# A latent-attention, delta-rule and expert layer on one core: gate factors made ahead of the applications, centred key weights

## The chip, the cores and the metric

One core of a Trainium2 chip runs the whole program in one launch. The metric is the device time of an execution in microseconds, as the median of several runs of the same kernel. All tensors are fp32. A product that needs more than one pass of TensorE is split: an operand becomes a high half (a ScalarE copy to `fp32r`) and a low half (VectorE or GpSimd subtracts), and three matmuls per product are made (lines 103 to 105).

## The reference

512 latent rows (8 batches of 64) attend to 8 x 1601 context rows; a gated delta rule follows, then a layer of 8 experts with 2 chosen per row. What the change touches:

```
# cross attention: keys of the context, 8 groups of 128, layer norm per group
k = LN(ctx @ Wk.T) * kxln_w + kxln_b          # mean and variance over the 128 of a group
scores = q @ k.T / sqrt(128); p = softmax(scores); o = p @ v

# delta rule, chunk of 64 = all rows of one batch; 32 value heads, 16 key heads, d = 128
q = l2norm(q) * 128**-0.5; k = l2norm(k); g = cumsum(gate)         # g: one value per row and head
decay = where(lower, exp(g[:,None] - g[None,:]), 0)
A     = where(strict, -(beta*k) @ k.T * decay, 0)
v_c   = solve(I - A) @ (beta*v)                                     # state is zero: one chunk
o     = where(lower, q @ k.T * decay, 0) @ v_c
out   = (rmsnorm(o) * norm_w * silu(z)) @ w_out
```

## The kernel before

The stages follow one another on each of the five queues: stage 1 (projections of the latents, 0 to 157 us of the profile), 1b (self attention and the loads for stage 3, to 201), 3 (cross attention, to about 1800), 4 (its projection), 5 (delta rule, 1850 to 2364), 7 (gate and output projection, to 2472), 8 (experts).

**Stage 1b** works in 8 lots. Per lot TensorE turns the probabilities (`self_turn_pe`), makes the scores of the lot three ahead and the values; VectorE (`s1b_dv`) takes sums and scaling of lot k+1, maxima and subtraction of lot k+3, and in lots 1 to 4 the low half of one quarter of the key weights `wkr`; ScalarE (`s1b_ac`) evicts probabilities and outputs, and in lots 0 to 3 writes the high half `wkh`. The first matmul of stage 3 waits for all of `wkl` and for lot 7.

**Stage 3** runs over 8 batches. In each, 13 tiles of up to 128 context rows are projected to 8 x 128 keys (24 matmuls of 128x512). `kx_stats_dv` (VectorE) takes `bn_stats` and `bn_aggr` per group and adds the epsilon; GpSimd raises to -0.5; `kx_norm_ac` normalises groups 0 to 3 on ScalarE (with `nmr` = -mean/std from `kx_nmr_dv`), `kx_norm_dv` groups 4 to 7 on VectorE, one instruction per group. Then TensorE turns the tile. Behind the 13 tiles stand 8 score blocks with softmax and values; the first tile of the next batch is laid between the last tiles and score block 0, and the values of block 0 wait for that tile's norm (`kn_ac`, `kn_dv`).

**Stage 5** is one written-out order of steps, `stage_order`, which all queues walk; each queue acts on the steps that are its own, in that order.

- 96 positions `mm`, each a chunk of 128 output columns: 64 convolution chunks and 32 gate chunks. ScalarE makes the high half, GpSimd (`qkv_split_po`, convolution chunks) or VectorE (`gz_split_dv`, gate chunks) the low half, two positions ahead. VectorE convolves with three instructions from PSUM.
- 32 `build`s of four heads. TensorE makes k.k and q.k, ScalarE scales them into `kqs`, GpSimd adds the mask `negm` and -g of the column's row to the row of gates in `gb`, ScalarE's `decay` takes exp, GpSimd multiplies the factor `b` (beta and norm) with k.k; VectorE's `second` writes q.k x decay into `aq` and b x decay into `at_of(n)`, which SP stores to `at_d` (`coupling_store`). `gb` is loaded by `gate_load`, a broadcast over 64 partitions of `gb_d`, in pairs of builds; `gb_d` holds g and b with 64 rows per run. Builds 0 to 15 come in four bursts at positions 42 to 76, builds 16 to 31 in the applications.
- Four solves, one per 64 systems, numbered 0 to 3: `system` loads the 32x32 diagonal blocks from `at_d`, VectorE makes 31 pairs of `tensor_tensor` (lines 2169, 2172), `solved` stores the inverses to `z_d`. Solve 0 and 1 run beside the positions, 2 and 3 in the applications.
- The applications: 32 groups of four heads in rounds t = 0 to 35. A group passes p0 (inverse blocks `xt`, fetched from `z_d`), p1 (coupling `mt`, fetched from `at_d`; VectorE adds), p2 (inverse again), p3 (`aq`), each 8 matmuls; group n makes p0 in round n, p1 in n+1, and so on. Between them lie the builds, solve steps (`some`, with a budget), `square` (sums of squares for the norm, ScalarE, four instructions with accumulator per group) and `rms`. p3 is scaled by `rq` and evicted by ScalarE for groups 0 to 19, by VectorE from 20 on.

The solve steps are paced so:

```
def some(steps, n):
    while n > 0 and (step := next(steps, None)) is not None:
        yield step
        n -= 180 + step[2] * (32 - step[2])
```

## Time and profile before

| | |
|---|---|
| runs | 2776.19, 2776.43, 2780.57 us (median 2776.43) |
| profiled execution | 2779.4 us; its span 2777.6 us, granted TensorE clock 0.982 |
| busy | PE 2646.0 us (95%), DVE 1861.7 (67%), ACT 1574.0 (57%), POOL 504.8 (18%) |
| DMA | 317.91 MB, 116 GB/s of HBM traffic over the span; 128712 of 255061 packets under 512 B |
| chain that ended last | PE 79%, DVE 10%, ACT 4%, the rest issue, DMA and queues |

PE is TensorE's matmuls, PEld its weight loads, DVE VectorE, ACT ScalarE, POOL GpSimd, SP the queue that issues nearly all transfers. A row's line (L2169) is that of the kernel; `cv<-at_d` at L1815 is the load of the systems (they lie in a part of `cv`), `lnw` at L2169 is the solve's scratch. Busy time says little by itself; the question at each place is which wait ends last.

### The profile page before, as it was taken

How to read it: one execution, taken by the hardware profiler on the slowest of the kernel's cores; microseconds unless marked ns; L12 is line 12 of the kernel's file. 1: busy time of each engine (PE TensorE's matmuls, PEld its weight loads, DVE VectorE, ACT ScalarE, POOL GpSimd, SP SyncE). 2: the span in 40 equal slices, each digit the busy share in tenths (PEclk: the TensorE clock that was granted, in tenths of full speed). 3: DMA queues.
4: the chain of work that ended last, by engine and by line, in shares of the span. 5: the costliest groups of instructions: out<-in, count | busy, mean ns of one | idle time of the engine just before them, and what ended most of it. 6: DMA issues, size and time to landing. Idle time of an engine off the chain costs nothing.

```text
span 2777.6 us, 39649 instructions
## 1 busy us (share of the span) xinstructions
PE 2646.0 (95%) x13810; PEld 2194.4 (79%) x13810; DVE 1861.7 (67%) x4737; ACT 1574.0 (57%) x2992; POOL 504.8 (18%) x428
## 2 busy tenths in 40 slices
PE   6889999999999999999999999999999879999999
PEld 5778788887887887887887887878877768777887
DVE  7747648548547557457466476668669866668997
ACT  7945436436436445445345355437676567857776
POOL 4402002002002012011011020005353332022111
PEclk9989999999999999999999999999999999989999
DMA  3433013022022031031030121445676642549996
GB/s 125 137 123 86 10 55 93 15 67 75 17 79 61 20 88 46 24 94 30 24 99 20 40 84 50 132 140 156 177 211 168 158 94 66 187 184 368 376 371 228
DMA packets 255061, 317.91 MB, mean 114 GB/s; under 512 B 128712, under 2 KB 166216, under 8 KB 241808
## 3 DMA queue, kind: packets, MB, share of 16 engines
q1 hardware_dynamic: 251392, 310.03, 36.0%
q0 software_dynamic: 3040, 5.08, 0.7%
q8 instruction: 112, 1.84, 0.3%
q14 instruction: 85, 0.70, 0.1%
q10 hardware_dynamic: 432, 0.27, 0.0%
HBM read 274.22 MB, written 46.98 MB: 116 GB/s over the span
## 4 chain that ended last, share of the span: by engine, by line
PE 79%; DVE 10%; ACT 4%; issue 2%; DMA 2%; POOL 1%; SPq 1%; POOLq 0%; DVEq 0%; ACTq 0%
PE ps L103 20%; PE ps L105 20%; PE ps L104 20%; PE ps L874 3%; PE ps L830 3%; PE ps L902 2%; DVE lnw L2169 2%; DVE zz L2172 2%; PE ps L855 1%; DVE cv L2136 1%; PE ps L895 1%; PE ps L1344 1%; PE ps L1343 1%; PE ps L2010 1%; PE ps L579 1%
## 5 line engine op out<-in xcount | busy, mean ns | idle before, releaser
L1244 POOL TENSOR_TENSOR lnw<-lnw,half 128x8 f32<-128x8 f32 x88 | 144.4, 1641 | 1217.6 <-DVE lnw L964 1217.6
L103 PE MATMUL ps<-whf,cth 128*128 128x512 f32 (+1 forms) x832 | 336.1, 404 | 1.8 <-ACT kn L1117 1.8
L103 PE MATMUL ps<-cnh,pth 128*128 128x512 f32 (+1 forms) x832 | 329.9, 397 | 6.4 <-issue 6.4
L105 PE MATMUL ps<-whf,ctl 128*128 128x512 f32 (+1 forms) x832 | 325.9, 392 | 0.0
L104 PE MATMUL ps<-cnl,pth 128*128 128x512 f32 (+1 forms) x832 | 324.9, 390 | 0.0
L104 PE MATMUL ps<-wlf,cth 128*128 128x512 f32 (+1 forms) x832 | 324.9, 390 | 0.0
L105 PE MATMUL ps<-cnh,ptl 128*128 128x512 f32 (+1 forms) x832 | 324.6, 390 | 0.0
L2662 DVE TENSOR_TENSOR ml<-mr,mh 128x2048 fp32r<-128x2048 f32 x90 | 203.3, 2286 | 26.5 <-ACT mh L2604 26.5
L1155 ACT ACTIVATE pr<-ps,sm 128x1601 f32<-128x1601 f32 x56 | 89.6, 1600 | 205.7 <-DVE sm L1017 205.7
L1180 ACT ACTIVATE xo<-ps 128x128 f32<-128x128 f32 x64 | 17.7, 277 | 312.9 <-PE ps L902 312.9
L1036 DVE TENSOR_TENSOR ptl<-ps,pth 128x512 fp32r<-128x512 f32 (+1 forms) x256 | 139.1, 585 | 78.8 <-ACT pth L1167 78.4
L959 DVE BATCH_NORM_STATS2 lnw<-ps 128x6 f32<-128x128 f32 (+1 forms) x832 | 175.7, 282 | 17.1 <-PE ps L105 17.1
L103 PEld LDWEIGHTS ps<-cnh,pth 128*128 128x128 f32 (+1 forms) x832 | 156.3, 188 | 38.6 <-ACT kn L1117 7.9
L105 PEld LDWEIGHTS ps<-whf,ctl 128*128 128x128 f32 (+1 forms) x832 | 153.1, 184 | 37.6
L105 PEld LDWEIGHTS ps<-cnh,ptl 128*128 128x128 f32 (+1 forms) x832 | 156.2, 188 | 33.3
L104 PEld LDWEIGHTS ps<-cnl,pth 128*128 128x128 f32 (+1 forms) x832 | 156.6, 188 | 30.9
L103 PEld LDWEIGHTS ps<-whf,cth 128*128 128x128 f32 (+1 forms) x832 | 153.4, 184 | 34.5 <-issue 3.5
L104 PEld LDWEIGHTS ps<-wlf,cth 128*128 128x128 f32 (+1 forms) x832 | 153.7, 185 | 31.6
L2136 DVE SCALAR_TENSOR_TENSOR cv<-ps,cw,cv 128x504 f32<-128x504 f32 (+2 forms) x192 | 140.8, 733 | 46.5 <-ACT cv L1895 41.9
L103 PE MATMUL ps<-xh,wqh 128*128 128x512 f32 x384 | 158.8, 413 | 9.6 <-DVE wql L2080 9.4
L2604 ACT ACTIVATE mh<-mr 128x2048 fp32r<-128x2048 f32 x90 | 165.8, 1917 | 0.0
L1001 DVE TENSOR_TENSOR cnl<-pr,cnh 128x512 fp32r<-128x512 f32 (+1 forms) x104 | 71.9, 691 | 126.1 <-ACT cnh L1138 126.1
(349 smaller groups left out, 6421.5 us busy)
## 6 DMA issues: line engine op xcount, KB each, us to landing
mr<-in_moe SPq DMA_DIRECT2D x90, 1024.0 KB, 7.2
ctr<-in_ctxt SPq DMA_DIRECT2D x96, 256.0 KB, 3.0
pr<-in_ctxn SPq DMA_DIRECT2D x96, 256.0 KB
wv<-in_wv SPq DMA_DIRECT2D x64, 256.0 KB, 2.8
wr<-in_wqkv SPq DMA_DIRECT2D x64, 256.0 KB, 3.0
...
```

The source lines that it names most:

```text
L103: pe.matmul(dst, lh, rh, start=first, stop=False)
L104: pe.matmul(dst, lh, rl, start=False, stop=False)
L105: return pe.matmul(dst, ll, rh, start=False, stop=last)
L830: f = pe.transpose(bank(4 + p)[:, 128 * g:128 * g + w], src[0:w, 4 * p + g, :], ident[0:w, 0:w])
L874: f = pe.transpose(bank(4 + w % 2)[0:n, 128 * (i % 4):128 * (i % 4) + 128], pr[:, s, o:o + n], ident)
L959: t = vs(dv.bn_stats(bns[0:w, s, g, :], src[:, 128 * g:128 * g + 128]))
L1036: dv.tensor_tensor(ptl[0:n, 4 * w:4 * w + q, :], src, pth[0:n, 4 * w:4 * w + q, :].bitcast(fp32), ALU.subtract).then_inc(p_low, 1)
L1155: ac.activation(pr[:, s, :], ps[:, 0:SC], ACT.Exp, scale=SCALE, bias=nb[:, s:s + 1], accum_out=rsum[:, s:s + 1]).then_inc(p_exp, 1)
L1244: po.tensor_tensor(rs[0:w, s, :], nv[0:w, s, :], half[0:w, 0:8], ALU.pow).then_inc(kx_rs, 1)
L2136: f = dv.scalar_tensor_tensor(dst[:, :, j:64], src[:, :, 0:64 - j], cw[:, 4 * c + 3 - j:4 * c + 4 - j], dst[:, :, j:64], ALU.mult, ALU.add)
L2604: ac.activation(mh[:, q % 6, :], mr[:, q % RAW, :], ACT.Copy).then_inc(mo_high.sem, 1)
L2662: dv.tensor_tensor(ml[:, q % 6, :], mr[:, q % RAW, :], mh[:, q % 6, :].bitcast(fp32), ALU.subtract).then_inc(mo_low.sem, 1)
```

## The change

- Stage 1b: `center_wk_dv` takes, for each quarter of the key weights, the mean over each group's 128 columns off them, in lots 0 to 3; ScalarE's high half waits for it. Projected keys then have mean zero.
- Stage 3: the variance comes from the `bn_stats` halves by four small instructions instead of `bn_aggr`; `nmr` and its semaphore go; ScalarE normalises with a scale alone, VectorE four groups in one instruction.
- Stage 5, positions: `gb_d` gets a third row per head, the query scale `rq` (one more transpose, a wider eviction, two stores), with the rows of a head side by side. In four bursts at s = 44, 53, 62, 71 a long tile `pg` (16 heads x 3 rows x 64) is loaded, masked and shifted, put through exp, multiplied and stored to `cf_d`: the factors of builds 16 to 31. `mt` and `xt` share its memory and are cleared at s = 80 instead of 38.
- Stage 5, applications: builds 16 on have no GpSimd step and no `decay`; `gate_load` reads them from `cf_d`; `second` multiplies in two dependent instructions. p3 of groups 16 on needs no scale. `square` from group 8 on is one ScalarE instruction and a VectorE reduce. Solve budgets, the rounds of `solved` (0 for 4), `system` (4 for 5), the second solve (5 for 6), the third (16 for 15), builds (two a round till round 3) and the squares (from round 8, one in two rounds, from 24 two a round) move.

```diff
-        gb_d = dram("gb_d", [128, 2, 128])
+        gb_d = dram("gb_d", [2, 128, 3, 64])
+        cf_d = dram("cf_d", [4, 128, 2048])
...
+        def center_wk_dv(dv, c):
+
+            raw = wkr[:, c, :].rearrange("p (g d) -> p g d", g=8)
+            if c == 0:
+                dv.wait_ge(d_wv, 16)
+            t = vs(dv.tensor_reduce(mv[:, c, :, 0], raw, AX.X, ALU.add))
+            dv.wait_ge(dv_step, t)
+            dv.scalar_tensor_tensor(raw, mv[:, c, :, 0].unsqueeze(2).to_broadcast([128, 8, 128]), -1.0 / 128.0, raw,
+                                    ALU.mult, ALU.add).then_inc(wk_centered.sem, 1)
...
+                if k == 0:
+                    center_wk_dv(dv, 0)
                 if 1 <= k < 5:
+                    if k < 4:
+                        center_wk_dv(dv, k)
...
-                    if k == 0:
-                        ac.wait_ge(d_wv, 16)
+                    ac.wait_ge(*wk_centered.at(k + 1))
...
-            dv.wait_ge(dv_step, t)
-            for g in range(lo, hi):
-                t = vs(dv.bn_aggr(mv[0:w, s, g, :], bns[0:w, s, g, :]))
-            dv.wait_ge(dv_step, t)
-            dv.tensor_scalar(nv[0:w, s, lo:hi], mv[0:w, s, lo:hi, 1], 1e-5, None, ALU.add).then_inc(kx_var, 1)
+            apart, square = mv[0:w, s, lo:hi, 0], mv[0:w, s, lo:hi, 1]
+            dv.wait_ge(dv_step, t)
+            t = vs(dv.tensor_tensor(apart, bns[0:w, s, lo:hi, 1], bns[0:w, s, lo:hi, 4], ALU.subtract))
+            vs(dv.scalar_tensor_tensor(nv[0:w, s, lo:hi], bns[0:w, s, lo:hi, 2], 128.0 * 1e-5, bns[0:w, s, lo:hi, 5],
+                                       ALU.add, ALU.add))
+            dv.wait_ge(dv_step, t)
+            t = vs(dv.scalar_tensor_tensor(square, apart, 0.25, apart, ALU.mult, ALU.mult))
+            dv.wait_ge(dv_step, t)
+            dv.scalar_tensor_tensor(nv[0:w, s, lo:hi], nv[0:w, s, lo:hi], 1.0 / 128.0, square, ALU.mult, ALU.add).then_inc(kx_var, 1)
...
-            for g in range(4, 8):
-                f = dv.tensor_scalar(dst[0:w, g, :], src[:, 128 * g:128 * g + 128], mv[0:w, s, g, 0:1],
-                                     rs[0:w, s, g:g + 1], ALU.subtract, ALU.mult)
-            f.then_inc(kn_dv, 1)
+            dv.tensor_tensor(dst[0:w, 4:8, :], src[:, 512:1024].rearrange("p (g d) -> p g d", g=4),
+                             rs[0:w, s, 4:8].unsqueeze(2).to_broadcast([w, 4, 128]), ALU.mult).then_inc(kn_dv, 1)
...
+                burst, r = divmod(s - 44, 9)
+                if 0 <= burst < 4:
+                    if r == 0:
+                        yield "pg_load", burst, 0
+                    if r in (2, 3):
+                        yield "pg_mask", burst, r - 2
+                    if r == 4:
+                        yield "pg_exp", burst, 0
+                    if r in (5, 6):
+                        yield "pg_scale", burst, r - 5
+                    if r == 7:
+                        yield "pg_store", burst, 0
+                if s == 80:
+                    yield "clear", 0, 0
...
-                yield from some(steps, 400 if t < 3 else 700)
+                yield from some(steps, 500 if t < 12 else 700)
                 if 0 <= t - 1 < 32:
                     yield "p1", t - 1, 0
-                for _ in range(2 if t < 3 else 1):
+                for _ in range(2 if t < 4 else 1):
                     if todo:
                         yield from building(todo.pop(0))
-                if t == 13:
+                if t == 12:
                     yield from built()
                 if 0 <= t - 2 < 32:
                     yield "p2", t - 2, 0
-                yield from some(steps, 400 if t < 3 else 800 if t < 15 else 1000)
+                yield from some(steps, 400 if t < 12 else 800)
                 if 0 <= t - 3 < 32:
                     yield "p3", t - 3, 0
-                if t in (4, 14, 22):
+                if t in (0, 14, 22):
                     yield from steps
-                    solved_to = (4, 14, 22).index(t) + 1
+                    solved_to = (0, 14, 22).index(t) + 1
                     yield "solved", solved_to, 0
-                if t in (6, 15):
-                    steps = solving(2 if t == 6 else 3)
+                if t in (5, 16):
+                    steps = solving(2 if t == 5 else 3)
                 while fetched < 16 and 2 * fetched <= t + 3 and fetched // 4 <= solved_to:
                     yield "fetch", fetched, 0
                     fetched += 1
-                if t in (5, 14):
+                if t in (4, 14):
                     yield "system", solved_to + 1, 0
                 if t >= 2 and t % 2 == 0 and t // 2 + 1 < 16:
                     yield "fetch_coupling", t // 2 + 1, 0
-                if squares <= t - 4 and squares < 28:
-                    yield "square", squares, 0
-                    squares += 1
-                    if squares % 2 == 0:
-                        yield "rms", squares // 2 - 1, 0
+                for _ in range(2 if t >= 24 else 1 if 8 <= t and t % 2 == 0 else 0):
+                    if squares < 28:
+                        yield "square", squares, 0
+                        squares += 1
+                        if squares % 2 == 0:
+                            yield "rms", squares // 2 - 1, 0
...
+            if m >= 8:
+                sp.wait_ge(*d_cf.at(16 * ((m - 8) // 2 + 1)))
             for b in range(2):
-                sp.dma_start((gb2 if core_over(m) else gb)[64 * b:64 * b + 64, f:f + 2, :, :, :].rearrange("p f h a t -> p (f h) a t"),
-                             gb_d[8 * m:8 * m + 8, :, 64 * b:64 * b + 64].unsqueeze(0).to_broadcast([64, 8, 2, 64])).then_inc(d_gb[m % 4].sem, 16)
+                dst = (gb2 if core_over(m) else gb)[64 * b:64 * b + 64, f:f + 2, :, :, :]
+                if m >= 8:
+                    sp.dma_start(dst.rearrange("p f h a t -> p (f h a t)"),
+                                 cf_d[(m - 8) // 2, 64 * b:64 * b + 64, 1024 * (m % 2):1024 * (m % 2) + 1024]).then_inc(d_gb[m % 4].sem, 16)
+                else:
+                    sp.dma_start(dst.rearrange("p f h a t -> p (f h) (a t)"),
+                                 gb_d[b, 8 * m:8 * m + 8, 0:2, :].rearrange("h a t -> h (a t)").unsqueeze(0).to_broadcast([64, 8, 128])).then_inc(d_gb[m % 4].sem, 16)
+
+        def factor_load(sp, k):
+
+            sp.wait_ge(d_gt, 32)
+            if k > 0:
+                sp.wait_ge(*d_cf.at(16 * k))
+            for b in range(2):
+                sp.dma_start(pg[64 * b:64 * b + 64, :, :, :].rearrange("p h a t -> p (h a t)"),
+                             gb_d[b, 64 + 16 * k:80 + 16 * k].rearrange("h a t -> (h a t)").unsqueeze(0).to_broadcast([64, 3072])).then_inc(d_pg.sem, 16)
+
+        def factor_store(sp, k):
+            sp.wait_ge(*pg_scaled.at(4 * k + 4))
+            sp.dma_start(cf_d[k].rearrange("p (h c) -> p h c", h=16),
+                         pg[:, :, 0:2, :].rearrange("p h a t -> p h (a t)")).then_inc(d_cf.sem, 16)
...
-                    po.wait_ge(d_gt, 16)
+                elif step == "pg_mask":
+                    e = pg[:, 8 * k:8 * k + 8, 0, :]
+                    po.wait_ge(*d_pg.at(32 * (n + 1)))
+                    po.tensor_tensor(e, e, negm.unsqueeze(1).to_broadcast([128, 8, 64]), ALU.add).then_inc(pg_masked.sem, 2)
+                    m = 4 * n + 2 * k
+                    po.wait_ge(*pg_masked.at(8 * n + 4 * k + 2))
+                    po.tensor_tensor(e, e, ngc[:, 2 + m // 8, 4 * (m % 8):4 * (m % 8) + 8].unsqueeze(2).to_broadcast([128, 8, 64]),
+                                     ALU.add).then_inc(pg_masked.sem, 2)
+                elif step == "pg_scale":
+                    e, b, r = pg[:, 8 * k:8 * k + 8, 0, :], pg[:, 8 * k:8 * k + 8, 1, :], pg[:, 8 * k:8 * k + 8, 2, :]
+                    po.wait_ge(*pg_exp.at(n + 1))
+                    po.tensor_tensor(b, b, e, ALU.mult).then_inc(pg_scaled.sem, 1)
+                    po.tensor_tensor(e, e, r, ALU.mult).then_inc(pg_scaled.sem, 1)
+                elif step == "clear":
+                    po.wait_ge(*d_cf.at(64))
                     po.memset(mt[:, :, :, :], 0.0).then_inc(zeroed.sem, 1)
                     po.memset(xt[:, :, :, :], 0.0).then_inc(zeroed.sem, 1)
...
+                    else:
+                        dv.wait_ge(*aq_out.at(n + 1))
+                        kk, over = (kqs[:, n % 4, :].rearrange("p (k a t) -> p k a t", k=2, a=2)[:, :, a, :] for a in range(2))
+                        t = vs(dv.tensor_tensor(over, pair(b)[:, :, 1, :], kk, ALU.mult))
+                        dv.wait_ge(dv_step, t)
+                        dv.tensor_tensor(kk, pair(b)[:, :, 0, :], kk, ALU.mult).then_inc(at_out.sem, 1)
...
+                    if n < 16:
+                        dv.tensor_tensor(vb[:, j, h:h + 4, :], src, rq[:, j, h:h + 4].unsqueeze(2).to_broadcast([128, 4, 128]),
+                                         ALU.mult).then_inc(apD_dv.sem, 1)
+                    else:
+                        dv.tensor_scalar(vb[:, j, h:h + 4, :], src, 1.0, None, ALU.mult).then_inc(apD_dv.sem, 1)
+                elif step == "square" and n >= ALONE:
+                    hd = 4 * (n % 8)
+                    dv.wait_ge(*o_squared.at(n - ALONE + 1))
+                    dv.tensor_reduce(sso[:, n // 8, hd:hd + 4], gz[:, n % 3, :].rearrange("p (h d) -> p h d", h=4),
+                                     AX.X, ALU.add).then_inc(sso_out.sem, 1)
```

## Rows read from the trace of the kernel before

**Rows 1.** By stretches: us, PE, PEld, DVE, ACT, POOL busy (instructions), PEclk, DMA share, GB/s
```profile
2110.00:2130.00 20.00, 18.39 (x92) 14.56 (x90) 19.09 (x35) 15.57 (x37) 8.61 (x8) 1.00 0.62 184
2200.00:2240.00 40.00, 30.24 (x238) 27.21 (x237) 23.76 (x44) 21.86 (x80) 20.27 (x28) 0.87 0.90 181
2240.00:2300.00 60.00, 45.07 (x361) 41.85 (x362) 45.76 (x116) 36.19 (x154) 20.19 (x20) 0.94 0.29 60
2300.00:2365.00 65.00, 58.17 (x506) 56.58 (x504) 39.11 (x87) 49.31 (x192) 13.34 (x8) 1.00 0.30 78
```

**Rows 2.** Timeline of PE, one batch change: start, us, what, [idle before <-releaser]
```profile
484.63 0.47 PE L103 MATMUL ps<-whf,cth 128*128 128x512 f32 x1 [0.25 <-ACT kn L1117]
...
497.24 0.47 PE L103 MATMUL ps<-cnh,pth 128*128 128x512 f32 x1 [0.92 <-issue]
```

**Rows 3.** Timeline of DVE: end of solve 1, start of solve 2
```profile
2204.28 0.19 DVE L2172 TENSOR_TENSOR zz<-zz,lnw 128x31 f32<-128x31 f32 x1
...
2242.75 0.20 DVE L2169 TENSOR_TENSOR lnw<-cv,zz 128x31 f32<-128x31 f32 x1 [7.23 <-DMA cv<-at_d]
```

**Rows 4.** Timeline of SP's DMA issues: loads of the third system
```profile
2238.22 2.30 SPq L1815 DMA_DIRECT2D cv<-at_d  x4
```

**Rows 5.** Chain that ended last, second half of the applications
```profile
2284.01 2.75 DMA z_d<-zz
...
2294.63 0.22 DVE lnw L2169
...
2320.84 2.64 DMA z_d<-zz
...
2327.54 1.16 PE ps L2052 x8
```

**Rows 6.** Timeline of ACT in the applications
```profile
2251.42 0.42 ACT L1908 ACTIVATE gb<-gb 128x256 f32<-128x256 f32 x1 [8.28 <-POOL gb L1969]
```
**Rows 7.** Timeline of DVE in the same batch change
```profile
495.78 1.36 DVE L993 TENSOR_SCALAR kn<-ps,lnw 128x128 f32<-128x128 f32 x4
```

**Rows 8.** Groups by form, 1850 to 2365 us (the delta rule)
```profile
L1983 POOL TENSOR_TENSOR wql<-wr,wqh 128x512 fp32r<-128x512 f32 x64 | 83.6, 1307 | 330.9 <-ACT wqh L1831 330.9
...
L1965 POOL TENSOR_TENSOR gb<-gb,cst 128x256 f32<-128x256 f32 x32 | 26.4, 826 | 7.5 <-DMA gb<-gb_d 7.5
L1972 POOL TENSOR_TENSOR gb<-gb,kqs 128x256 f32<-128x256 f32 x32 | 25.5, 798 | 33.0 <-ACT kqs L1902 32.8
...
L2152 DVE TENSOR_TENSOR aqA<-gb,kqs 64x256 f32<-64x256 f32 x32 | 14.8, 463 | 3.5 <-ACT gb L1908 3.3
...
L2186 DVE TENSOR_TENSOR vb<-ps,rq 128x512 f32<-128x512 f32 x12 | 8.3, 691 | 12.6 <-PE ps L2074 12.6
```

**Rows 9.** Groups by form, 150 to 205 us: shapes, count, busy us, mean ns
```profile
L604 DVE TENSOR_REDUCE asum<-pm 128x8 f32<-128x512 f32 x8 | 5.4, 678 | 0.0
...
L637 DVE TENSOR_TENSOR wlf<-wvf,whf 128x1024 fp32r<-128x1024 f32 x4 | 4.9, 1216 | 0.0
```

**Rows 10.** Chain that ended last, end of stage 1b: start, us, what
```profile
184.03 0.60 PE ps L568 x4
...
197.91 3.06 PE ps L579 x16
```

**Rows 11.** Timeline of POOL in the projections
```profile
2136.39 1.30 POOL L1983 TENSOR_TENSOR wql<-wr,wqh 128x512 fp32r<-128x512 f32 x1 [9.10 <-ACT wqh L1831]
```

**Rows 12.** Timeline of DVE at the same moment
```profile
2136.52 1.34 DVE L2169 TENSOR_TENSOR lnw<-cv,zz 128x156 f32<-128x156 f32 x1
2137.90 0.32 DVE L2172 TENSOR_TENSOR zz<-zz,lnw 128x156 f32<-128x156 f32 x1
```

**Rows 13.** Timeline of PE in the projections: its stalls behind DVE
```profile
2094.15 0.50 PE L103 MATMUL ps<-xh,wqh 128*128 128x512 f32 x1 [1.42 <-DVE wql L2080]
...
2104.65 0.79 PE L103 MATMUL ps<-xh,wqh 128*128 128x512 f32 x1 [2.33 <-DVE wql L2080]
...
2130.96 0.50 PE L103 MATMUL ps<-xh,wqh 128*128 128x512 f32 x1 [2.57 <-DVE wql L2080]
```

115 lines of the change are left out of this document (65 added, 50 removed).

## The prediction

> **What bounds the kernel now.** I read the page's slices first: TensorE is 8 to 9 tenths busy nearly everywhere, at full clock, so only its gaps can be won. Then the table by stretches for the delta rule's applications: from 2200 to 2365 us TensorE is idle 9.8 + 14.9 + 6.8 = 31.5 us [rows 1], the largest hole that the diff touches. The timeline of TensorE shows what the diff's other part can win: in each of seven batch changes of the cross attention it waits 0.25 and 0.92 us for a normalised key tile, and nowhere else in the batch [rows 2].
>
> Three queues in the applications decide the end. VectorE solves the triangular systems serially; solve 1 ends at 2204.5, solve 2 starts only at 2242.75 because it waited 7.2 us for its system from DRAM [rows 3], whose loads SP issued at 2238.2 [rows 4]. Solve 2 ends at 2284.0, its store and the next loads take till 2294.6, solve 3 runs till 2320.8, and the applications of the last quarter start at 2327.5 [rows 5]. ScalarE meanwhile waits up to 8.3 us for GpSimd's masks [rows 6], since GpSimd's queue also holds `rms`, which waits for VectorE. So the chain is VectorE's solves plus what stands between them, not TensorE.
>
> **Part A, centred key weights.** Stage 3: VectorE's four `tensor_scalar` of 128x128 (1.36 us together, [rows 7]) become one `tensor_tensor` PSUM x broadcast of 128x512; the same form takes 0.69 us in the applications [rows 8], line 2186. `nmr` goes (0.15 us on the queue), and ScalarE no longer waits for it. Eight `bn_aggr` and one add become four small instructions, two of them dependent: between 0.3 us won and 0.1 lost per tile; I take nothing for half tiles. The 0.92 us wait ends with that normalisation, so it shrinks by 0.7 to 0.8; the 0.25 us wait goes wholly, as VectorE, GpSimd and ScalarE all come about 1 us earlier. That is 7 x 1.05 = 7.4 us, plus 0.8 us in the last batch, where the same chain of normalise, turn, score has no other work beside it: **-8.2 us**. In the other 190 us of a batch TensorE is full; there it is worth nothing.
>
> The price stands in stage 1b. VectorE gets four times a reduce and a `scalar_tensor_tensor` of 128x1024. The reduce of 128x512 took 0.68 us and a two-input instruction of 128x1024 1.22 us [rows 9]; with 0.53 us for 512 more columns the reduce is 1.2, the pair with its wait 2.4 us, four pairs 9.6 us. Is it covered? TensorE ends stage 1b 12 us after VectorE (chain: turn of lot 5 at 184.0, last values 197.9 + 3.1 = 201.0 [rows 10]), which looks like cover. But before lot 5 VectorE has no idle time: its cycle per lot (maxima, sums, scale, low half) sums to 4.0 us, as long as TensorE's. The diff puts the pairs into lots 0 to 3, so the probabilities of lot 5 come 9.6 us later, and the 17 us of lots 5 to 7 still follow (each a round of turn, evict, values). ScalarE now waits for each centred chunk ahead of evicting the next lot's probabilities, which adds to it. Bounds 0 (all in the tail) and 11; I take **+9.5 us**, by the count of VectorE's queue. A together: +1.3 us.
>
> **Part B, the applications.** For builds 16 to 31 three GpSimd instructions of 128x256 (0.83 and 0.80 us [rows 8], the third somewhat shorter) and ScalarE's `exp` leave; VectorE's coupling product becomes two dependent ones of 128x128, so `second` is about 0.46 x 2 [rows 8] + 0.55 = 1.45 us instead of 1.4. Gate loads from the eighth pair on read 4 KB runs, not 256 B ones. GpSimd no longer lies in the loop, so ScalarE's waits of [rows 6] go; next late is VectorE itself. In order:
>
> - Solve 1's last 10 us ran beside GpSimd's masks; undisturbed it is some 4 us shorter, and the first applications start near 2201.
> - Builds 16 to 24 now end in round 5, the system's loads move from round 5 to 4. VectorE has 9 x 1.45 + 5 x 0.69 = 16.5 us ahead of solve 2; TensorE has some 17 us, with its start-up at low clock. That is 2218 to 2220. The loads then need SP and 4.5 us [rows 3, 4]: 2223, and I give 3 us for SP's queue: solve 2 starts at 2226, not 2242.75: -17 us.
> - Solve 2 with seven `second` and eight sums: 22 us of solve (solve 3 took 26.2 with seven sums of 0.6) + 10 + 5 = 37 to 40 us, before 41: -1 us.
> - From its end everything is as before: 11.0 us of store and loads, solve 3 26.2 us, 6.7 us of store and fetch, then TensorE's 3.57 us per group [rows 5].
> - Squares move behind round 24 and become, from group 8 on, one ScalarE instruction per group in place of eight, plus a VectorE reduce of 0.68 us. Two groups per round: VectorE 2 x 0.68 + 0.69 + 0.69 = 2.7 us, under TensorE's 3.57. Nothing, unless the round slips. Groups 16 to 19 leave by one ScalarE copy; ScalarE isn't on the chain.
>
> B together: **-18 us**; bounds -10 (no gain from the earlier system but the undisturbed VectorE and shorter loads) and -24.
>
> **Part C, the factors made ahead, in the projections.** Four bursts, each two loads of 0.79 MB, eight GpSimd instructions of 128x512, one `exp` of 128x1024 on ScalarE with one or two table loads, and a store of 1 MB; also the clearing of `mt` and `xt` moves from before the bursts to behind them, where it waits for the last store. A GpSimd `tensor_tensor` of 128x512 takes 1.31 us [rows 8]: 10.5 us a burst, 42 in all. GpSimd itself has room (busy under 60% there), SP issues eight loads and four stores more (under 6 us), and the weights' loads queue behind 2.6 MB per 27 us; queued behind them are weight splits with some 4 us of slack. ScalarE's `exp` waits for masks; behind it are evictions with about 9 us of slack.
>
> What isn't covered is VectorE. A solve instruction of 128x156 took 1.34 us when GpSimd's 1.30 us split had started just before it, 0.32 us right after [rows 11, 12]. From 2080 to 2145 VectorE is about 95% busy (19.1 of 20 us in the slice of [rows 1]) and TensorE stalls for it three times, 1.4, 2.3 and 2.6 us [rows 13]. Bursts 3 and 4 fall there: 21 us of GpSimd. Half of VectorE's work reads PSUM and wasn't stretched; one VectorE instruction still gets in per GpSimd instruction. So about 5 us per burst, less 2 us of slack after it: **+8 us**, bounds 0 and 24 (below).
>
> The Trainium skill (SBUF — State Buffer, "Who interferes with whom") says that a GpSimd instruction holds the shared read interface for its whole length and that a VectorE instruction with two SBUF inputs waits it out. By that rule, with which the trace agrees in [rows 11, 12], the long rows are charged in full wherever VectorE has such work, and the sum would be that of rival 3.
>
> **Sum.** The profiled execution took 2779.4 us, 3.0 over the median of 2776.43. 2779.4 + 1.3 - 18 + 8 = 2770.7; on the scale of the median **2767.7 us**.
>
> **Rivals.**
> 1. *The centring is covered.* VectorE ends stage 1b 12 us before TensorE; if the tail absorbs the pairs, A is -8.2: 2758.2. Against it: no idle VectorE time between lots 0 and 4. 0.16.
> 2. *The applications' chain only moves to SP and DMA.* Eight query and key loads of 512 KB and the coupling stores still go ahead of the system's loads; in 2200 to 2240 the DMA engines were 90% busy [rows 1]. If solve 2 starts only 8 us earlier, B is -10: 2775.7, no change. For it: the issue waits in this stretch; against it: twelve gate loads with a thousand short packets each become long runs. 0.20.
> 3. *Slower: GpSimd's long rows stop VectorE throughout the projections.* Price: 57% of VectorE's time there are two-input SBUF instructions; 42 x 0.57 = 24 us, all passed to TensorE through late weight splits as in [rows 13]. 2767.7 + 16 = 2783.7. It decides from 23 us on. Against it: bursts 1 and 2 have VectorE only 55 to 80% busy. 0.12. The rule of the Trainium skill quoted above is this mechanism.
>
> That the change wouldn't do what it says is excluded by the diff: the factors are read from DRAM, and no GpSimd step is left for builds 16 on.
>
> **How the numbers follow.** The forecast has 0.48 (its own range 2762 to 2774), rivals 0.16, 0.20, 0.12; 0.04 lies outside. A measurement of this kernel can tell 0.2%, 5.5 us: faster is under 2770.9, slower over 2782.0. Faster: three quarters of the forecast (0.355), rival 1 (0.155), a third of rival 2 (0.06), 0.02: 0.59. Slower: most of rival 3 (0.09), a little of 2 and of the rest: 0.12. The same: 0.29. Range 2755 to 2780: it leaves out the lower end of rival 1 and most of 3.
>
> **What would show it.** Stage 3's first projection matmul starts near 210, not 201; batch period 197.8 us instead of 198.8; the waits of [rows 2] under 0.15 us. VectorE instructions over 1 us beside GpSimd ones between 2010 and 2130, more TensorE stalls for `wql`. Solve 2 starts some 26 us after the end of solve 1, not 38, no GpSimd but `rms` after 2195, and the last quarter starts about 117 us after the first application (2192.7), not 134.8. Wrong if stage 1b doesn't grow, if stalls in the projections exceed 15 us, or if the 7 us wait for the third system stays.

## The result, and the profile after

The change makes the kernel slower. The median after is 2807.51 us (2805.47 to 2808.80, 4 runs), before 2778.50 us in the same session (2776.19 to 2781.27, 4 runs): ratio 1.0104, interval 1.0092 to 1.0116, so about 29 us. Forecast were 2767.7 us and at most 2780.

| | before | after |
|---|---|---|
| profiled execution, its span | 2779.4, 2777.6 us | 2806.5, 2804.7 us |
| granted TensorE clock | 0.982 | 0.976 |
| PE / DVE / ACT / POOL busy | 2646.0 / 1861.7 / 1574.0 / 504.8 us | 2653.8 / 1780.8 / 1523.3 / 509.5 us |
| first application (first `p0` matmul) starts | 2192.7 | 2233.5 |
| last `p0` group starts | 2353.4 | 2379.7 |

VectorE and ScalarE have less to do than before, and the kernel is longer. The two starts divide the difference of the spans, 27.1 us, by part. Stage 5's first weight load is issued at 1846.49 instead of 1849.25: **A**, -2.8. From there to the first application it takes 43.6 us longer: **C** (with what the order does there). From the first to the last `p0` group it takes 146.2 instead of 160.7 us: **B**, -14.5. Behind it +0.8.

Each part is read from one execution, and the border between C and B moves from one to the next. In the traces of four other kernels whose stage 5 is the one from before the change (the `centred_` kernels below), the way of C takes 344.6 to 346.8 us (before 343.5, after 387.0) and the stretch of B 155.5 to 159.4 us (before 160.7, after 146.2). So C costs 40 to 44 us, and B gains 9 to 15.

**Where A's price and gain are.** The chain that ended last, end of stage 1b (answers to [rows 10]), then the timeline of DVE in a batch change (to [rows 7]):

```profile
187.35 1.24 DVE wvf L632
...
205.88 3.06 PE ps L580 x16
208.94 0.72 PE ps L104
```
```profile
492.20 0.69 DVE L1001 TENSOR_TENSOR kn<-ps,lnw 65x512 f32<-65x512 f32 x1 [0.90 <-POOL lnw L1243]
```

The last values end at 208.94 instead of 200.97, 8.0 us later. In a batch change the one instruction in place of four takes 0.69 us instead of 1.36. The two waits of [rows 2] are gone: TensorE has no idle time from 480 to 500, and a batch takes 197.2 instead of 198.8 us.

**Where B's gain is.** The chain that ended last, in the applications (answers to [rows 5]), and DVE's start of solve 2 (to [rows 3]):

```profile
2306.29 2.65 DMA z_d<-zz
...
2344.49 3.26 DMA z_d<-zz
...
2351.06 2.08 PE ps L2131 x8
```
```profile
2238.37 0.19 DVE L2262 TENSOR_TENSOR zz<-zz,lnw 128x31 f32<-128x31 f32 x1
...
2269.24 0.21 DVE L2259 TENSOR_TENSOR lnw<-cv,zz 128x31 f32<-128x31 f32 x1 [6.99 <-DMA cv<-at_d]
```

Solve 2 starts 30.7 us after the end of solve 1 (38.3 before) and lasts to 2306.29, 37.0 us; the last quarter starts 117.5 us after the first application instead of 134.8.

**Where C's loss is.** The same 220 us of both kernels, the projections with the bursts and nothing of the applications, by the view of stretches (columns as in [rows 1]); the first fence is the kernel before:

```profile
1970.00:2190.00 220.00, 210.37 (x1046) 166.72 (x1045) 163.61 (x298) 152.30 (x352) 82.42 (x82) 0.98 0.67 183
```
```profile
1970.00:2190.00 220.00, 184.19 (x861) 142.35 (x861) 147.30 (x232) 142.86 (x308) 118.25 (x110) 0.90 0.72 200
```

TensorE works 26.2 us less and at a lower mean clock; 861 matmul records stand where 1046 stood. DVE is less busy as well (147 against 164 us): it waits too. Only POOL and the DMA engines have more. The table of waits, 1985 to 2215 us, says whom TensorE waits for (in total, times, longest):

```profile
POOL wql L2060 <- ACT wqh L1885: 46.3, 11, 6.9
POOL pg L2021 <- DMA pg<-gb_d: 39.7, 4, 12.5
ACT wqh L1885 <- DMA wr<-in_wqkv: 30.4, 6, 7.1
...
PE ps L104 <- POOL wql L2060: 20.1, 5, 7.5
...
PE ps L104 <- DVE wql L2159: 9.0, 5, 3.1
...
PE ps L2087 <- ACT cv L1912: 6.6, 2, 3.4
```

TensorE's waits for VectorE's low halves are 9.0 us, what they were before (9.4 in the kernel before). New are 20.1 us behind GpSimd's and 6.6 us behind ScalarE (its silu of a convolution chunk, which TensorE turns); together they are the 26 us of additional idle time. Upstream stand two waits for transfers, one on GpSimd (39.7 us) and one on ScalarE (30.4 us; 5.3 before). Burst 1 shows how they stand in line. The timelines of POOL, of ACT and of PE:

```profile
2017.38 1.30 POOL L2060 TENSOR_TENSOR wql<-wr,wqh 128x512 fp32r<-128x512 f32 x1
2026.14 1.29 POOL L2021 TENSOR_TENSOR pg<-pg,cst 128x512 f32<-128x512 f32 x1 [7.47 <-DMA pg<-gb_d]
...
2030.17 1.04 POOL L2024 TENSOR_TENSOR pg<-pg,ngc 128x512 f32<-128x512 f32 x1
2031.17 1.46 POOL L2060 TENSOR_TENSOR wql<-wr,wqh 128x512 fp32r<-128x512 f32 x1
```
```profile
2026.56 0.63 ACT L1885 ACTIVATE wqh<-wr 128x512 fp32r<-128x512 f32 x1 [3.02 <-DMA wr<-in_wqkv]
...
2028.72 1.28 ACT L1965 ACT_TABLE_LOAD   x1
2031.24 1.06 ACT L1965 ACTIVATE pg<-pg 128x1024 f32<-128x1024 f32 x1 [1.23 <-POOL pg L2024]
```
```profile
2032.68 0.79 PE L104 MATMUL ps<-xh,wqh 128*128 128x512 f32 x1 [5.58 <-POOL wql L2060]
```

SP issued the burst's load at 2014.15 and the next weight chunk at 2015.45; the chunk, 256 KB, landed 11.1 us later, where half of the chunks before the change took under 3.2. In the other bursts the chunk right behind the load took 11.7, 12.3 and 11.1 us. So the high half starts at 2026.56. GpSimd was idle 7.5 us for the load, then works 5 us on masks (four instructions), and only at 2031.17, 4 us after its input was there, comes the low half; TensorE has stood still for 5.58 us. The list of DMA issues (KB each, median us to landing) has the load itself:

```profile
wr<-in_wqkv SPq DMA_DIRECT2D x27, 256.0 KB, 4.4
...
pg<-gb_d SPq DMA_DIRECT2D x8, 768.0 KB, 10.0
```

Burst 2 shows the second way to TensorE, through ScalarE's queue; the timelines of ACT and of PE:

```profile
2064.90 0.63 ACT L1885 ACTIVATE wqh<-wr 128x512 fp32r<-128x512 f32 x1 [5.74 <-DMA wr<-in_wqkv]
2065.55 1.28 ACT L1912 ACT_TABLE_LOAD   x1
2066.84 0.63 ACT L1912 ACTIVATE cv<-cv 128x512 f32<-128x512 f32 x1
```
```profile
2067.53 1.12 PE L2087 MATMUL ps<-cst,cv 128*128 128x128 f32 x4 [3.44 <-ACT cv L1912]
2070.74 0.80 PE L104 MATMUL ps<-xh,wqh 128*128 128x512 f32 x1 [2.10 <-POOL wql L2060]
```

The late chunk holds the high half, and behind the high half the silu stands that TensorE's transposes need.

And a stall costs more than its length. TensorE's stretches around this stall (PE busy, granted clock, DMA share, GB/s):

```profile
2060.00:2064.00 4.00, 4.00 (x19) 1.00 0.93 214
2064.00:2068.00 4.00, 0.56 (x3) 0.84 0.77 294
2068.00:2072.00 4.00, 1.90 (x7) 0.50 0.04 7
2072.00:2076.00 4.00, 4.00 (x10) 0.50 0.61 173
2076.00:2080.00 4.00, 4.00 (x21) 0.88 0.92 269
```

From 2064 TensorE is idle for 5.5 us in two pieces; the granted clock falls to its lower level, 1.2 GHz, in between and is back only after 2076. In the four full microseconds from 2072 the view counts only 10 matmuls, against 19 in the four from 2060.

### The profile page after: what moved, and what is told of

It reads as the page before. It is cut to its first block, busy times and chain, and to the rows that moved or that the text cites. A ratio compares the mean times of both kernels' runs of the same rounds, so it can differ in the third digit from the quotient of the medians.

```text
span 2804.7 us, 38656 instructions
## 1 busy us (share of the span) xinstructions
PE 2653.8 (95%) x13811; PEld 2202.1 (79%) x13811; DVE 1780.8 (63%) x3893; ACT 1523.3 (54%) x2834; POOL 509.5 (18%) x412
## 4 chain that ended last, share of the span: by engine, by line
PE 79%; DVE 8%; DMA 5%; ACT 4%; issue 2%; POOL 1%; SPq 1%; POOLq 0%; ACTq 0%; DVEq 0%
PE ps L104 20%; PE ps L106 20%; PE ps L105 20%; PE ps L888 3%; PE ps L844 3%; PE ps L916 2%; DMA wr<-in_wqkv 2%; PE ps L869 2%; DVE lnw L2259 1%; PE ps L909 1%; DVE zz L2262 1%; PE ps L1347 1%; PE ps L1346 1%; DVE cv L2215 1%; PE ps L2131 1%
## 5 line engine op out<-in xcount | busy, mean ns | idle before, releaser
L104 PE MATMUL ps<-xh,wqh 128*128 128x512 f32 x384 | 164.3, 428 | 32.3 <-POOL wql L2060 20.1
L623 ACT ACTIVATE cth<-ctr 128x512 fp32r<-128x512 f32 (+1 forms) x104 | 63.0, 613 | 211.3 <-PE ps L106 211.3
L615 DVE TENSOR_TENSOR ctl<-ctr,cth 128x512 fp32r<-128x512 f32 (+1 forms) x104 | 69.2, 671 | 161.4 <-ACT cth L623 161.4
```

The lines of the kernel that those rows point to most:

```text
L104: pe.matmul(dst, lh, rh, start=first, stop=False)
L615: dv.tensor_tensor(ctl[:, n % 2, :, 0:w], ctr[:, n % 3, :, 0:w], cth[:, n % 2, :, 0:w].bitcast(fp32), ALU.subtract).then_inc(ct_low, 1)
```

## The experiments

All times are given as distance to the kernel before on the same chip, (ratio - 1) x 2778.6 us; the changed kernel itself stands at **+28.9**. An interval of 0.0010 to 0.0017 on either side is 3 to 5 us. The experiments ran on five chips, so a difference between two of them carries both intervals. `one_burst` and every kernel with "short" in its name leave out part of the computation.

### The size of C: one burst instead of four

```diff
                 burst, r = divmod(s - 44, 9)
-                if 0 <= burst < 4:
+                if burst == 0:
...
-                sp.wait_ge(*d_cf.at(16 * ((m - 8) // 2 + 1)))
+                sp.wait_ge(*d_cf.at(16))
```

> Part C's size. Only the first of the four bursts is left (loads, masks, exp, products, store of bursts 2 to 4 left out; builds 20 to 31 read the first burst's factors, so part of the computation is left out). In the changed kernel the way from stage 5's start to the first application is 43 us longer than before the change and the whole kernel 29 us slower. If part C carries that (all theories), three quarters of 43, so 25 to 35 us, come back: time near 2775, ratio to the kernel before 0.997 to 1.002, first application near 2203 instead of 2233.5. If it came from elsewhere (the system's load at round 4, the solve order, the third transpose), under 8 us come back: ratio over 1.007.

2770.69 us, ratio 0.9973 (0.9960 to 0.9985), **-7.5**: 36.4 us came back, just over the 25 to 35 expected, and the first application starts at 2201.0. C it is, 12 us a burst; and at that rate the rest of the change, with no burst left, would be worth some 20 us (an estimate; no such kernel was run).

### The load

```diff
-                sp.dma_start(pg[64 * b:64 * b + 64, :, :, :].rearrange("p h a t -> p (h a t)"),
+                n = 16 if k == 0 else 1
+                sp.dma_start(pg[64 * b:64 * b + 64, 0:n, :, :].rearrange("p h a t -> p (h a t)"),
```

> Bursts 2 to 4 load one head of sixteen instead of all (2 x 49 KB instead of 2 x 786 KB), every other instruction and wait is kept (part of the computation left out). Theory 1, the transfer: the burst's load keeps the 16 DMA engines busy for some 10 us, the weight chunk behind it lands 11 to 12 us after its issue instead of 4.4, and GpSimd waits up to 12.5 us for the load with weight splits behind it; then 6 to 10 us per burst come back, 18 to 30 in all, ratio to before 1.000 to 1.004, and the GpSimd wait for pg falls from 39.7 us to about 15. Theory 2, GpSimd's long rows stop VectorE: nothing comes back, ratio 1.009 to 1.012. Theory 3, ScalarE's exp and its table loads: the same as theory 2.

Ratio 1.0048 (1.0031 to 1.0065), **+13.3**: the load is worth 15.6 us for three bursts, under theory 1's 18 to 30 and far from the nothing of theories 2 and 3. In the three bursts with short loads the chunk right behind the load landed after 4.9, 5.4 and 3.9 us, in the first after 11.1, and TensorE no longer waits for ScalarE. In the table of waits those of TensorE for GpSimd fell, those for VectorE rose:

```profile
PE ps L104 <- DVE wql L2160: 21.9, 6, 7.2
...
POOL pg L2022 <- DMA pg<-gb_d: 14.6, 4, 7.5
...
PE ps L104 <- POOL wql L2061: 5.6, 2, 4.3
```

### GpSimd's rows

```diff
-                    e = pg[:, 8 * k:8 * k + 8, 0, :]
+                    w = 64 if n == 0 else 2
+                    e = pg[:, 8 * k:8 * k + 8, 0, 0:w]
```

> In bursts 2 to 4 the eight GpSimd instructions work on 2 of 64 columns (128x16 instead of 128x512, part of the computation left out), all loads and waits kept. Theory 1: only GpSimd's own 31 us of work less behind the wait, the late weights remain; 3 to 10 us come back, ratio 1.007 to 1.010. Theory 2: 20 to 30 us come back, ratio 1.000 to 1.003. Theory 3: under 3 us, ratio 1.010.

Ratio 1.0063 (1.0046 to 1.0079), **+17.5**: 11.4 us, just above theory 1's 3 to 10 us and about half of theory 2's 20 to 30. GpSimd's busy time falls by 24.6 us (from 1970 to 2210 us, 122.1 to 97.5), so somewhat less than half of it was on the way.

### Masks two rounds later

```diff
-                    if r in (2, 3):
-                        yield "pg_mask", burst, r - 2
-                    if r == 4:
+                    if r in (4, 5):
+                        yield "pg_mask", burst, r - 4
+                    if r == 6:
```

> The load stays where it is, GpSimd's masks and everything behind them move two rounds (some 11 us) later: GpSimd does not stand in front of the load with weight splits behind it. It splits theory 1. Theory 1a, the blocked GpSimd queue: its 39.7 us of waits fall under 8 and 4 to 7 us per burst come back, 15 to 25 in all, ratio 1.001 to 1.005. Theory 1b, the weight chunk behind the load in the DMA queues: it is as late as before, ScalarE's 30 us of waits for weights stay, under 8 us come back, ratio 1.008 to 1.010. Theories 2 and 3: no change, ratio 1.010.

Ratio 1.0062 (1.0045 to 1.0079), **+17.2**: 11.7 us for four bursts, between the under 8 of theory 1b and the 15 to 25 of theory 1a. GpSimd no longer waits for the load at all, but most of ScalarE's waits for weights stay (23.5 of 30.4 us), and the low halves are now late on VectorE:

```profile
ACT wqh L1885 <- DMA wr<-in_wqkv: 23.5, 5, 8.5
PE ps L104 <- DVE wql L2159: 23.4, 6, 5.8
```

### Load and rows together, then ScalarE's exp too

`short_both` joins the two edits; `short_all` has this besides:

```diff
+                    if n == 0:
                         ac.activation(pg[:, :, 0, :], pg[:, :, 0, :], ACT.Exp).then_inc(pg_exp.sem, 1)
+                    else:
+                        ac.activation(pg[:, :, 0, 0:2], pg[:, :, 0, 0:2], ACT.Copy, scale=0.0).then_inc(pg_exp.sem, 1)
```

> Bursts 2 to 4 with short loads and with GpSimd's short rows together (one head of sixteen loaded, 2 of 64 columns worked on; part of the computation left out). The two alone gave back 15.5 and 11.5 us of the 36.5 that leaving the three bursts out gave back. If transfers and rows are two separate costs, both together give back 27: ratio to before 1.000 to 1.002. If they are one queue in which either is enough to be late (GpSimd's stream of weight splits, late by the wait or by the work), together they give back under 20: 1.003 to 1.005. If each hides behind the other, over 32: under 0.999.

> The same, and ScalarE's exp of 128x1024 in bursts 2 to 4 is a copy of 128x32 (part of the computation left out), so its 1.1 us and the table loads around it (1.28 us each) go. Theory 3, ScalarE: the 5 to 10 us that are still open between short_both and one_burst (0.9973) come back here, ratio 0.997 to 0.999. If the store of 1 MB and the waits alone keep the rest, under 3 us come back against short_both.

1.0008 (0.9999 to 1.0018), **+2.2**, and 0.9980 (0.9971 to 0.9990), **-5.6**. Both lie where the first case of their expectation has them. Load and rows together give back 26.7 us, alone they gave 15.6 and 11.4, sum 27.0: within the intervals they add up. The exp with its table loads is 7.8 more, and 1.9 us, less than an interval, are left for the stores and waits. So three bursts cost 26.7 + 7.8 + 1.9 = 36.4 us, and no single theory holds: the load, GpSimd's rows and ScalarE's exp each delay the weight chunks by a part of their own length.

By which engine the rows' 11.4 us reach TensorE isn't separated. With the loads short, TensorE's waits for VectorE's low halves are 21.9 us beside long rows (`short_loads`) and 12.3 us beside short ones (`short_both`), those for GpSimd's 5.6 and 8.1: there it is VectorE, whose low halves take 993 ns in the mean beside the long rows and 876 beside the short.

### What of the load costs

> late_masks (masks two rounds later) and short_loads (one head of sixteen loaded in bursts 2 to 4, part of the computation left out) together. Alone they stand at 1.0062 (-11.5 us against the changed kernel) and 1.0048 (-15.5). If GpSimd's wait for the load is the whole cost of the load, one of the two is enough and both together give no more than short_loads: ratio 1.004 to 1.005. If the weight chunk behind the load costs as well, late_masks has kept that part and loses it now: both together 1.003 to 1.004. If the two gains are of different things (the later masks move GpSimd's rows away from the builds' own), they add up: 27 us, 1.000 to 1.002.

Ratio 1.0028 (1.0018 to 1.0039), **+7.8**, just under the second case's 1.003 to 1.004. With GpSimd's wait already out of the way, the short loads still give 9.4 us; with the masks in their old place they gave 15.6. That speaks for the weight chunks behind the load as somewhat more than half of its cost and GpSimd's wait as the rest; the difference, 6.2 us, is near the intervals.

### Another queue, and pieces

`act_queue` lets ScalarE issue the load, `pieces` cuts it into four of 4 heads each:

```diff
-                elif step == "pg_load":
-                    factor_load(sp, i)
...
+                elif step == "pg_load":
+                    factor_load(ac, n)
```
```diff
-                    if r == 0:
-                        yield "pg_load", burst, 0
+                    if r < 4:
+                        yield "pg_load", burst, r
```

> late_masks with the bursts' loads issued by ScalarE instead of SyncE, so that the weight chunk behind them is in another queue. Theory 1b as an order in SyncE's queue: the weights land 4 to 5 us after their issue again, ScalarE's waits for weights fall from 23.5 to about 8 us, 8 to 12 us come back against late_masks (1.0062), ratio 1.002 to 1.003. Theory 1b as a share of the 16 engines, which are busy all the same: weights land after 8 us and more, ratio 1.005 to 1.008, ScalarE paying some 1 us per issue.

> late_masks with each burst's load cut into four pieces (4 heads, 2 x 196 KB), one behind the weight chunk of each of four positions. The bytes are the same, but no chunk has over 0.4 MB ahead of it: the transfer of a chunk and a piece fits a position of 5.5 us. Theory 1b: ScalarE's waits for weights fall under 10 us and 8 to 12 us come back against late_masks: ratio 1.002 to 1.003. Theory 2 or 3: the same as late_masks, 1.006.

> The kernel of pieces once more, since its four runs lay between 2787.8 and 2797.3 us. If the cut load earns nothing over late_masks: ratio 1.006 again. If it earns what its profiled execution showed (first application at 2217 instead of 2227): 1.003, and the four runs were on the high side.

The other queue: 1.0095 (1.0078 to 1.0112), **+26.4**, 9 us worse than `late_masks` and outside both expectations. The chunk right behind the load landed 9.4, 9.3, 7.4 and 8.0 us after its own issue, in `late_masks` 11.1, 11.7, 10.2 and 10.8. But in three of the four bursts it was issued 3 to 4 us after the load instead of 1.2 to 1.3; counted from the load's issue it came after 10.3, 12.5, 11.3 and 12.1 us instead of 12.4, 12.9, 11.4 and 12.0, hardly earlier. ScalarE's waits for weights fell from 23.5 to 17.1 us, the issue costs ScalarE 1.1 us a burst, and TensorE's waits for the low halves stayed (22.4 us for VectorE's, 6.3 for GpSimd's). Why the median lost 9 us isn't shown by the trace: its profiled execution, 2799 us, was at the low end of its four runs. The Trainium skill (DMA: Bandwidth & Descriptors, "Queues, rings and completion order") says that each DMA engine goes round between the queues it has work for. In this trace a chunk in a queue of its own still took over twice its usual 3.2 us beside the load.

Pieces: 1.0061 (1.0044 to 1.0078) and, again, 1.0053 (1.0039 to 1.0066): **+14.7** to **+17**, at most 2.5 us under `late_masks`. The expected 8 to 12 us did not come. ScalarE's waits for weights fell to 16.6 and 14.5 us (expected under 10), but the last piece is issued only one position ahead of the masks, and GpSimd waits for it again, 24.4 and 21.7 us where `late_masks` had none. So the two runs don't show whether it is the bytes that cost or the length of the single load.

### A alone, and its price

> The kernel before with part A alone (centred key weights; no part B, no part C). The trace of the changed kernel puts A at -2.8 us: stage 1b's end 8.0 us later, 1.6 us won in each of seven batch changes. Theory: ratio 0.9985 to 0.9995, first projection of stage 3 at 209, batch period 197.2 us. If A's price or gain depends on the rest (stage 5 and later do not touch it), it would be elsewhere; none of the 29 us of loss comes from A in any theory, so over 1.001 would be a surprise.

2774.85 us, ratio 0.9987 (0.9978 to 0.9996), **-3.6**: as the trace had it (-2.8).

In `centred_in_tail` the pairs, ScalarE's copies and the low halves stand behind the sums of lot 7 (and ScalarE's copies in its rounds 5 to 7 and behind the last output):

```diff
-                if k == 0:
-                    center_wk_dv(dv, 0)
...
+            for k in range(6):
+                if k < 4:
+                    center_wk_dv(dv, k)
```

> centred_only with the four pairs of reduce and subtraction (and ScalarE's copies and the low halves behind them) taken out of lots 0 to 4 and put behind the sums of lot 7, where VectorE has nothing left to do while TensorE still works 12 us on lots 5 to 7. It tests that the price of A was the place, not the work: VectorE has 9.7 us of pairs, 4.9 us of low halves and 1.4 us of context splits from about 183 on, so it is ready near 199, and stage 3 starts at 201 to 202 instead of 209. Expected 7 to 8 us under centred_only, ratio 0.9955 to 0.997. If ScalarE's copies now wait in front of lot outputs, 3 us of it are lost: 0.998.

Ratio 0.9980 (0.9971 to 0.9989), **-5.6**, not -11: the expectation's second case. The last values end at 204.2 (before 201.0, `centred_only` 209.4), but then TensorE waits: each chunk goes VectorE, ScalarE, VectorE, and ScalarE's last copy stood behind the last lot's output:

```profile
205.15 1.05 ACT L686 ACTIVATE whf<-wvf 128x1024 fp32r<-128x1024 f32 x1
206.23 1.23 DVE L649 TENSOR_TENSOR wlf<-wvf,whf 128x1024 fp32r<-128x1024 f32 x1 [2.96 <-ACT whf L686]
...
208.11 0.80 PE L103 MATMUL ps<-whf,cth 128*128 128x512 f32 x1 [3.92 <-DVE ctl L613]
```

Next the subtraction went to GpSimd, which is idle there:

```diff
+            dv.tensor_scalar(mv[:, c, :, 0], mv[:, c, :, 0], -1.0 / 128.0, None, ALU.mult).then_inc(wk_mean.sem, 1)
+        def s1b_po(po):
+            for k in range(5):
...
+                    po.tensor_tensor(raw, raw, mv[:, k, :, 0].unsqueeze(2).to_broadcast([128, 8, 128]),
+                                     ALU.add).then_inc(wk_centered.sem, 1)
...
+                    po.tensor_tensor(wkl[:, k - 1, :], wkr[:, k - 1, :], wkh[:, k - 1, :].bitcast(fp32),
```

> centred_only with VectorE left with the four sums of 128x1024 (1.2 us each) and a scaling of 128x8, while GpSimd, idle in stage 1b, does the four subtractions and the four low halves of the weights (128x1024, by the rows of 128x512 at 1.3 us each some 2.6 us, 21 us in all beside 30 us of lots). VectorE then has about as much as before the change, so lots 0 to 5 keep their pace. Theory (A's price is VectorE's queue): stage 3 starts at 201 to 203 instead of 209, 6 to 8 us under centred_only (0.9987): ratio 0.996 to 0.997, which beats both kernels. Rival: GpSimd's long rows of two inputs hold up VectorE's own two-input rows (its scaling of the probabilities), so half comes back: 0.9975 to 0.998. If nothing comes back, A's price is not VectorE's queue: 0.9985 to 0.999.

Ratio 0.9977 (0.9966 to 0.9987), **-6.4**, stage 3 starts at 205.5: the rival's half. The timelines of DVE and POOL show why (`centred_by_gpsimd`):

```profile
170.27 1.90 POOL L638 TENSOR_TENSOR wvf<-wvf,lnw 128x1024 f32<-128x1024 f32 x1 [31.57 <-DVE lnw L631]
...
171.05 1.67 DVE L608 TENSOR_TENSOR pm<-pm,asum 128x512 f32<-128x512 f32 x1
...
187.68 5.13 POOL L642 TENSOR_TENSOR wlf<-wvf,whf 128x1024 fp32r<-128x1024 f32 x2
...
190.46 2.90 DVE L608 TENSOR_TENSOR pm<-pm,asum 128x512 f32<-128x512 f32 x1
```

VectorE's scaling of the probabilities, 0.69 us alone, ends 0.55 us after GpSimd's instruction ends, all five times that it began beside one: it is held for all that is left of it. The last run keeps them apart: GpSimd's subtraction starts behind `mean_wk_dv`, and the low halves are VectorE's again, behind the sums of lot 7:

```diff
+                if k == 0:
+                    sum_wk_dv(dv, 0)
                 if k + 1 < 8:
                     self_sums_dv(dv, k + 1)
+                if k < 4:
+                    mean_wk_dv(dv, k)
                 if k + 3 < 8:
                     self_max_dv(dv, k + 3)
+                if k < 3:
+                    sum_wk_dv(dv, k + 1)
...
+            for k in range(6):
+                if k < 4:
+                    dv.wait_ge(wk_high, k + 1)
```

> centred_by_gpsimd with the order changed so that each of GpSimd's four subtractions (1.90 us) starts behind VectorE's scaling of a lot's probabilities and lies beside its maximum, its subtraction from PSUM and the next sum of 128x1024 (2.6 us), and with the four low halves on VectorE behind the sums of lot 7, beside TensorE's last lots. If the stretched rows (1.67 and 2.90 us against 0.69) were the rest of A's price, all of VectorE's scalings take 0.69 us again, stage 3 starts at 201 to 202 instead of 205.5, and 4 us more come back: ratio 0.996 to 0.997 (centred_by_gpsimd 0.9977). If VectorE's rows are stretched beside GpSimd whatever they read, the maxima and sums take over 1 us now and nothing comes back: 0.9975 to 0.998.

2770.62 us against 2781.04 us, ratio 0.9965 (0.9951 to 0.9979), **-9.7**; the first projection matmul starts at 201.85. This version beats both kernels. `centred_apart`, the same timelines:

```profile
168.21 0.69 DVE L607 TENSOR_TENSOR pm<-pm,asum 128x512 f32<-128x512 f32 x1
168.82 0.17 DVE L634 TENSOR_SCALAR lnw<-lnw 128x8 f32<-128x8 f32 x1
168.89 0.68 DVE L594 TENSOR_REDUCE am<-ps 128x8 f32<-128x512 f32 x1
...
169.06 1.90 POOL L640 TENSOR_TENSOR wvf<-wvf,lnw 128x1024 f32<-128x1024 f32 x1 [31.07 <-DVE lnw L634]
...
169.61 0.69 DVE L598 TENSOR_TENSOR pm<-ps,am 128x512 f32<-128x512 f32 x1
...
170.22 1.21 DVE L628 TENSOR_REDUCE lnw<-wvf 128x8 f32<-128x1024 f32 x1
```

The same 1.90 us of GpSimd lies beside a maximum, a subtraction from PSUM and a sum, and none of them is longer than without it. The run changed two things, the moment of the subtractions and the engine of the low halves; both took a GpSimd instruction away from beside the scaling.

### B without C, and with half of it

`order_only` has A and the new order of steps, with masks and exp of builds 16 to 31 inside the applications as before; `two_bursts` has `late_masks`' bursts for builds 16 to 23 and the old way for 24 to 31 (`order_only` has 16 in place of 24):

```diff
+        def made(n):
+            return 16 <= n < 24
...
-                elif step == "build" and n < 16:
+                elif step == "build" and not made(n):
```

> Parts A and B without C: the gates of builds 16 to 31 are loaded, masked on GpSimd and exponentiated on ScalarE inside the applications as before the change, but the order of steps (solve 1 ended at round 0, systems at rounds 4 and 14, two builds a round until round 3, later squares, outputs of groups 20 on by VectorE) is the new one. It splits B's 17.3 us. If the order earns them: -3 - 10 to 17 us, ratio 0.993 to 0.9955. If they are earned only since GpSimd has left the loop (it needs 2.35 us per build, 21 us for the nine builds ahead of the third system, and VectorE's in-order queue waits for it in front of sums of the applications): -3 to +5 us, ratio 0.999 to 1.002.

> late_masks with two bursts instead of four: factors of builds 16 to 23, on which the third system waits, made ahead, those of builds 24 to 31 made by GpSimd and ScalarE inside the applications as before. C costs 9.6 us per burst with late masks (38 us for four), so 19 for two. If the gain of B hangs on the first eight builds alone, B stays -14 to -17 and the sum is 2779.3 - 3 - 16 + 19: ratio 0.9995 to 1.001. If GpSimd's masks for the last eight hold up the last quarter too, B is -8: ratio 1.002 to 1.004.

`order_only` 0.9986 (0.9977 to 0.9995), **-3.9**: A's share alone, so the order by itself earns nothing; from the first to the last `p0` group it takes 159.2 us (155.5 to 160.7 in the kernels with the old stage 5, after 146.2). ScalarE again waits for GpSimd there:

```profile
2264.37 0.42 ACT L1970 ACTIVATE gb<-gb 128x256 f32<-128x256 f32 x1 [4.84 <-POOL gb L2054]
```

`two_bursts` 1.0017 (1.0007 to 1.0026), **+4.7**, just over the expected 0 to +3: the same stretch takes 149.8 us, so builds 16 to 23 carry most of B's gain (6 to 11 us by the traces), and two bursts cost more than that. GpSimd out of the loop with the old order of steps was not run.

## Why the prediction was wrong

**A.** Right in its mechanism and nearly in its price: +9.5 forecast, +8.0 measured; "by the count of VectorE's queue" was the right count. The gain was undersized: 7 x 1.05 forecast, 7 x 1.6 measured, since the waits of [rows 2] weren't all that depended on the normalisation; the 0.8 us for the last batch don't show. The net has the other sign: +1.3 forecast, -2.8 by the trace and -3.6 by the run of A alone.

**B.** Right in sign and nearly in size: -18 forecast, -17.3 at the start of the last quarter as predicted (117.5 us against "about 117"), of which 2.8 were given back inside it: -14.5, or 9 to 15 by all traces. That the end fits so well is in part luck, for two inner marks were off: solve 2 starts 30.7 us after solve 1, not 26, and the wait for its system stayed at 6.99 us, since SP issued those loads only at 2263.98. That wait was one of the prediction's own signs of being wrong; of the rival that the chain moves to SP and DMA this much is true. (The 11.0 us of store and loads between the solves are 10.6 by [rows 5]; nothing hangs on it.) That the gain needs GpSimd out of the loop, `order_only` shows.

**C.** This is the step that failed: **+8**, bounds 0 and 24, measured +40 to +44 by the traces, 12 us a burst by the runs. Three sentences of it:

- "the weights' loads queue behind 2.6 MB per 27 us; queued behind them are weight splits with some 4 us of slack" stood there and was costed at nothing, because the mean rate over 27 us left room (it is some 31 us: the kernel before issues 43 chunks from 2010 to 2160). But the 1.57 MB come at once: in burst 1 nothing that was issued behind them lands before 2026.5. 11.1 us against 3.2 us exceed the 4 us of slack by 4; ScalarE waited 3.0, 5.7, 5.9 and 5.6 us for the chunk behind the load in the four bursts. This is the larger part of the load's 15.6 us.
- "GpSimd itself has room (busy under 60% there)" looked at busy time. GpSimd's queue is in order: it waited 39.7 us for the loads, then worked 5 us on masks, with a low half of the weights behind both. This is a part of the load's cost and, as the waits of the changed kernel stand, of the rows' 11.4 us; which share of these comes through VectorE isn't separated. Work and waits in front of a queue entry that TensorE needs are not room.
- "ScalarE's `exp` waits for masks; behind it are evictions with about 9 us of slack": it costs 7.8 us for three bursts.

What was put down as the cost, "What isn't covered is VectorE", was not the one that came first: TensorE's waits for VectorE's low halves stayed at 9.0 us. Rival 3 gave the sign, 24 us of cost against some 42, and mostly from the wrong place. Its mechanism exists; the groups by form on DVE, 2005 to 2170 us, before, after and in `short_rows`:

```profile
L2080 DVE TENSOR_TENSOR wql<-wr,wqh 128x512 fp32r<-128x512 f32 x22 | 16.8, 764 | 6.3 <-ACT wqh L1831 6.3
```
```profile
L2159 DVE TENSOR_TENSOR wql<-wr,wqh 128x512 fp32r<-128x512 f32 x16 | 18.0, 1122 | 9.5 <-ACT wqh L1885 9.4
```
```profile
L2161 DVE TENSOR_TENSOR wql<-wr,wqh 128x512 fp32r<-128x512 f32 x17 | 18.2, 1072 | 8.6 <-ACT wqh L1885 8.6
```

The low halves took 1122 ns instead of 764, but with short rows 1072 all the same, and in the 220 us VectorE was busy 16 us less than before the change. The Trainium skill (SBUF — State Buffer, "Who interferes with whom") has the rule. By it an instruction of 0.69 us would end 0.69 us after GpSimd's; in `centred_by_gpsimd` it ended 0.55 us after, and in `centred_apart` those with one input in SBUF or none were left alone, so the timelines agree to 0.15 us. The price is paid where VectorE ends the wait: in stage 1b, and in `short_loads` once the weights are no longer late; in the changed kernel VectorE mostly waits itself.

**What wasn't in the sum at all** is the clock. Idle time and clock are separate losses: in the 220 us TensorE was idle 26.2 us more, and a matmul record took 0.214 us of busy time in the mean instead of 0.201 (184.19 / 861, 210.37 / 1046), which over 861 records is some 11 us. That is an estimate from the two rows of stretches, whose mean granted clocks are 0.90 and 0.98. A sum made of stall lengths would have been short by about a quarter even with the right stalls.

The range failed with C: its upper bound, 24 us, was that of one cause. Here three costs came from one burst and were added up. "Stalls in the projections exceed 15 us", a sign of being wrong, came true as well.

Open is why the median of `act_queue` lies 9 us above `late_masks`, through which engine GpSimd's rows cost their 11.4 us, and which share the lower clock has in the 12 us of a burst beyond the estimate above; no run separates these.
